# Causal mask by a product of constant rows, and row maxima of two heads at once, in a transformer block on one Trainium2 core

## What is computed

```python
xn = _layernorm(x, axis=-1)
q = (xn @ wq + bq).reshape(B, S, 16, 16); k = ...; v = ...
q = _apply_rope(q, cos, sin); k = _apply_rope(k, cos, sin)
scores = jnp.einsum('bhqd,bhkd->bhqk', q, k) / jnp.sqrt(jnp.float32(HEAD_DIM))
causal = jnp.where(jnp.tril(jnp.ones((S, S), jnp.float32)) == 0, -1000000000.0, 0.0)
attn = jax.nn.softmax(scores + causal, axis=-1)
s = jnp.einsum('bhqk,bhkd->bhqd', attn, v) -> (B, S, 256) @ wo + bo
g = _silu(((silu(xn @ wg.T) * (xn @ wu.T)) @ wd.T))
return x + s * g
```

## Time and profile before

| | us |
|---|---|
| median of 3 runs | 557.97 (557.56 to 561.14) |
| profiled execution: span | 562.5 |
| TensorE busy | 506.4 (90%) |
| VectorE busy | 461.9 (82%) |
| ScalarE, GpSimd busy | 332.2 (59%), 292.6 (52%) |

### The profile page before, as it was taken

One profiled execution on the slowest core, in us unless ns is written; L12 is line 12 of the kernel. 1 busy time (PEld: TensorE's weight loads), 2 busy tenths in 40 slices (PEclk: granted clock), 3 DMA queues, 4 the chain that ended last, 5 costly groups with the idle time before them and its releaser, 6 DMA issues.

```text
span 562.5 us, 11714 instructions
## 1 busy us (share of the span) xinstructions
PE 506.4 (90%) x3717; PEld 349.5 (62%) x3717; DVE 461.9 (82%) x1460; ACT 332.2 (59%) x682; POOL 292.6 (52%) x407
## 2 busy tenths in 40 slices
PE   0716989999999999979999999999999999999994
PEld 0614767566657677657866777676757775654753
DVE  3484897998799897976889897999799789998623
ACT  2257245676576657654586657674777556765750
POOL 2090059469263498344972499356854583422620
PEclk9977999999999999988999999999999999997996
DMA  5559624436307723383436733583436463652021
GB/s 194 183 157 241 120 71 140 116 98 166 67 4 197 196 65 115 116 176 109 108 123 145 195 63 115 149 182 110 134 101 151 113 173 115 128 124 60 4 77 38
DMA packets 47839, 69.47 MB, mean 124 GB/s; under 512 B 5496, under 2 KB 22776, under 8 KB 47776
## 3 DMA queue, kind: packets, MB, share of 16 engines
q1 hardware_dynamic: 46688, 67.62, 45.7%
q10 hardware_dynamic: 1088, 1.05, 0.6%
HBM read 38.11 MB, written 29.36 MB: 120 GB/s over the span
## 4 chain that ended last, share of the span: by engine, by line
PE 66%; DVE 15%; issue 5%; DMA 5%; SPq 4%; ACT 2%; POOL 2%; ACTq 0%; DVEq 0%; POOLq 0%
PE ps_w L544 36%; PE ps_w L556 15%; PE ps_o L648 10%; DVE ps_w L877 8%; PE ps_w L657 2%; SPq L517 2%; SPq L501 1%; DMA gate<-L_attn_wo 1%; ACT probs L767 1%; DVE row_max L877 1%; PE ps_w L663 1%; PE ps_w L569 1%; DMA k_st<-parts_k 1%; DVE high_low L865 1%; DVE hid L910 1%
## 5 line engine op out<-in xcount | busy, mean ns | idle before, releaser
L877 DVE CUSTOM_DVE_ANT_0 ps_w<-ps_w,cst 128x512 f32<-128x512 f32 (+3 forms) x512 | 235.3, 520 | 20.3 <-PE ps_w L556 19.4
L767 ACT ACTIVATE probs<-ps_w 128x512 f32<-128x512 f32 (+1 forms) x384 | 179.8, 535 | 63.8 <-PE ps_w L556 62.5
L959 POOL TENSOR_SCALAR_AFFINE_SELECT probs<-probs 128x256 f32<-128x256 f32 x256 | 108.5, 439 | 170.2 <-ACT probs L767 169.3
L544 PE MATMUL ps_w<-xt_hi,wgu_hi 128*128 128x512 f32 x192 | 84.1, 438 | 2.6 <-DVE row_max L877 1.1
L648 PE MATMUL ps_o<-probs,vals 128*32 128x512 f32 (+3 forms) x1024 | 84.6, 444 | 0.1
L556 PE MATMUL ps_w<-k_st,q_st 48*128 48x512 f32 (+3 forms) x512 | 80.0, 363 | 3.9 <-DMA k_st<-parts_k 1.8
L556 PE MATMUL ps_w<-q_st,k_st 52*128 52x512 f32 (+3 forms) x512 | 76.9, 354 | 4.4 <-DMA q_st<-minus_max 2.9
L544 PE MATMUL ps_w<-xt_lo,wgu_hi 128*128 128x512 f32 x192 | 76.8, 400 | 0.0
L556 PEld LDWEIGHTS ps_w<-k_st,q_st 48*128 48x128 f32 x512 | 45.0, 188 | 43.4 <-issue 28.1
L877 DVE DVE_READ_ACCUMULATOR2_ANT row_max<- 128x1 f32 x512 | 71.4, 139 | 0.0
L556 PEld LDWEIGHTS ps_w<-q_st,k_st 52*128 52x128 f32 x512 | 44.7, 187 | 32.4 <-issue 14.8
(11 more groups left out here) (98 smaller groups left out, 879.5 us busy)
## 6 DMA issues: line engine op xcount, KB each, us to landing
parts_q<-high_low SPq DMA_DIRECT2D x48, 256.0 KB, 3.1
q_st<-parts_q SPq DMA_DIRECT2D x64, 192.0 KB, 3.6
k_st<-parts_k SPq DMA_DIRECT2D x64, 192.0 KB, 4.6
parts_k<-high_low SPq DMA_DIRECT2D x42, 256.0 KB, 3.1
xn<-L_attn_x SPq DMA_DIRECT2D x8, 512.0 KB, 5.5
res<-L_attn_x SPq DMA_DIRECT2D x8, 512.0 KB, 4.0
q_st<-minus_max SPq DMA_DIRECT2D x256, 4.0 KB
result<-res SPq DMA_DIRECT2D x8, 512.0 KB, 5.1
```

Source lines behind the costliest of these rows:

```text
L544: last = pe.matmul(dst, w, m, start=(i == 0), stop=(i == len(terms) - 1))
L767: nc.scalar.activation(probs[:, (pair % 2) * SLOTS + slot, col:col + WIDTH[c]], w_of(kind, b, 3 * pair + c // 2, c % 2)[:, 0:WIDTH[c]], AC ...
L877: last = nc.vector.tensor_tensor_reduce(out=ps[:, col:col + w], in0=ps[:, col:col + w], in1=cst[:, C_MASK + SEQ - w:C_MASK + SEQ], scale=1 ...
L959: nc.gpsimd.affine_select(out=v, in_=v, compare_op=ALU.is_ge, fill=0.0, base=0, pattern=[[0, 2], [1, P]], channel_multiplier=-1).then_inc( ...
```

## The change

1. The mask of A is no longer added by VectorE. `causal` (128 by 384, constants, loaded as `mask_rows` and rounded once by ScalarE) has 64 rows for each head. In `masked_scores` every step of A ends with one more matmul per head, which adds the product of constant rows to the diagonal tile of each query tile: 128 columns in step 0, 256 in step 1 (both diagonals lie side by side), 128 in step 2. Both heads' banks are reported full together, by the last of these.
2. The maxima are plain `tensor_reduce` instructions. Where the two banks of a step are neighbours, one instruction takes both heads; else each head has its own. `a_taken` is raised once per step instead of once per bank, so both banks are let go together. TensorE's order and its banks are as before, but for the two heads the lower bank is the first now.
3. `row_max` is laid out so that its transpose holds 8 rows per head of a pair, MD needs 2 transfers of 8 rows each into one row of `q_st` per head, and B works with 49 rows. A row of ones in `k_st` (2 transfers at the start, from a memset) takes the place of the selector rows (8 transfers).
4. VectorE's list has 24 A items per batch instead of 48. The lists of TensorE, ScalarE, GpSimd and SyncE are the same.

```diff
 def scores / new masked_scores (TensorE)
+            def masked_scores(b, i):
+                pair, d = divmod(i, 3)
+                dst = [take_bank("A", b, i, 0), take_bank("A", b, i, 1)]
+                tiles, col_masked, masked = A_TILES[d]
+                for t, col in tiles:
+                    for h in range(2):
+                        pe.matmul(dst[h][:, col:col + (t + 1) * P], q_st[64 * h:64 * h + STACK, pair, t * P:(t + 1) * P],
+                                  k_st[64 * h:64 * h + STACK, pair, 0:(t + 1) * P], start=(col == 0), stop=False, skip_group_check=True)
+                for h in range(2):
+                    last = pe.matmul(dst[h][:, col_masked:col_masked + masked], causal[64 * h:64 * h + 64, 0:P],
+                                     causal[64 * h:64 * h + 64, P:P + masked], start=False, stop=True, skip_group_check=True)
+                done(last, "A")
...
+A_TILES = [([(3, 0)], 3 * P, P), ([(2, 0), (0, 3 * P)], 2 * P, 2 * P), ([(1, 0)], P, P)]
...
 B on TensorE
-                        need(pe, max_placed[g % 2], 128 * (2 * b + g // 2 + 1))
+                        need(pe, max_placed[g % 2], 32 * (2 * b + g // 2 + 1))
...
-                           lambda p, h, t, r: (q_st[64 * h:64 * h + r, p, t * P:SEQ], SEQ - t * P), STACK + 4)
+                           lambda p, h, t, r: (q_st[64 * h:64 * h + r, p, t * P:SEQ], SEQ - t * P), STACK + 1)
...
 MD on SyncE
-                    for tt in range(TT):
-                        for a in range(2):
-                            sp.dma_start(q_st[64 * a + STACK:64 * a + STACK + 4, 2 * i:2 * i + 2, tt * P:(tt + 1) * P].bitcast(F32),
-                                         minus_max[32 * tt:32 * tt + 4, i % 2:i % 2 + 1, :].bitcast(F32).broadcast_to([4, 2, P]))\
-                                .then_inc(max_placed[i % 2], 16)
+                    for a in range(2):
+                        row = q_st[64 * a + STACK:64 * a + STACK + 1, 2 * i:2 * i + 2, :].bitcast(F32).rearrange("o n (t c) -> o (n t) c", c=P)
+                        sp.dma_start(row, minus_max[32 * a:32 * a + 2 * TT, i % 2, :].bitcast(F32)).then_inc(max_placed[i % 2], 16)
...
 A on VectorE
-                    for h, qt, col in A_PARTS[c]:
-                        w = (qt + 1) * P
-                        hh = 2 * (pair % 2) + h
-                        last = nc.vector.tensor_tensor_reduce(
-                            out=ps[:, col:col + w], in0=ps[:, col:col + w], in1=cst[:, C_MASK + SEQ - w:C_MASK + SEQ],
-                            scale=1.0, scalar=-3e38, op0=ALU.add, op1=ALU.max, accum_out=row_max[:, g % 2, qt, hh:hh + 1])
+                    for t, col in A_TILES[d][0]:
+                        of_pair = row_max[:, g % 2, 0:64].rearrange("p (a c) -> p a c", a=2)[:, :, 4 * (pair % 2) + t]
+                        if second == first + 1:
+                            last = nc.vector.tensor_reduce(of_pair, ps_all[:, first:first + 2, col:col + (t + 1) * P], AX.X, ALU.max)
+                        else:
+                            for h, at in enumerate((first, second)):
+                                last = nc.vector.tensor_reduce(of_pair[:, h:h + 1], ps_w[at][:, col:col + (t + 1) * P], AX.X, ALU.max)
                     last.then_inc(a_taken, 1)
...
 the table of VectorE's order, one line of it
-        A12.6 A13.6 A14.6 A15.6 A16.6 A17.6 LO0.7 DN1.6 A18.6 A19.6 A20.6 A21.6 A22.6 A23.6 ON3.5 LO1.7 AT1.5 A24.6 A25.6 V0.7 A26.6
+        V1.7 A15.6 A16.6 G0.7 A17.6 U0.7 LO3.7 ON0.6 A18.6 HL0.7 A19.6 G1.7 A20.6 U1.7 G2.7 A21.6 OP0.5 A22.6 A23.6 U2.7 HL1.7 OP1.5 ON1.6
```

More of the change, by code:

```diff
@@ L45, in shape_constants, with causal_rows @@
     by_row = lambda t: np.tile(t.T, (HEADS, 1))
[L46 to L53, removed]
-    for a in range(2):
-        for s in range(2):
-            sel[4 * a + 2 * s + a, s, :] = 1.0
-    return sel.reshape(8, 2 * SEQ)
+    return np.concatenate([np.eye(P, dtype=np.float32), by_row(np.cos(freqs)), by_row(np.sin(freqs))], axis=1).astype(np.float32)
+def causal_rows():
+    of_q, of_k = np.zeros((P // 2, P), np.float32), np.zeros((P // 2, P), np.float32)
+    for r in range(P // 2):
+        of_q[r, 2 * r], of_q[r, 2 * r + 1] = 2.0 ** MASK_STEP, 2.0 ** -MASK_STEP
+        of_k[r, 2 * r] = -2.0 ** (-2 * MASK_STEP)
+        of_k[r, 2 * r + 1] = -2.0 ** (MASK_NEAR - MASK_STEP)
+        of_k[r, 2 * r + 2:] = -2.0 ** (MASK_NEAR + MASK_STEP)
+    return np.concatenate([np.tile(of_q, (2, 1)), np.tile(of_k, (2, 2))], axis=1)
 B_PARTS = [[(h, kt, col) for kt, col in part] for part in ([(0, 0)], [(1, 0), (3, 384)], [(2, 0)]) for h in range(2)]
-A_PARTS = [[(h, TT - 1 - kt, col) for h, kt, col in part] for part in B_PARTS]
+A_TILES = [([(3, 0)], 3 * P, P), ([(2, 0), (0, 3 * P)], 2 * P, 2 * P), ([(1, 0)], P, P)]
 WIDTH = [SEQ, SEQ, SEQ, SEQ, SEQ // 2, SEQ // 2]
@@ L186 @@
[L186 to L189, removed]
@@ L255, in __init__, with build @@
             assert len(banks) == WORK[kind][1]
-            for j, at in enumerate(banks):
-                full[first] += 1
-                kinds[kind] = kinds.get(kind, 0) + 1
+            for j, at in enumerate(sorted(banks) if kind == "A" else banks):
+                if j == 0 or kind != "A":
+                    full[first] += 1
+                    kinds[kind] = kinds.get(kind, 0) + 1
                 self.of[kind, b, i, j] = (at, full[first], seen.get(at))
                 seen[at] = (kind, kinds[kind])
-def build(nc, x, wq, bq, wk, bk, wv, bv, wo, bo, w_gate, w_up, w_down, consts, selectors, out):
+def build(nc, x, wq, bq, wk, bk, wv, bv, wo, bo, w_gate, w_up, w_down, consts, mask_rows, out):
     with ExitStack() as ctx:
@@ L301, in build @@
         k_st = sb("k_st", [P, PAIRS, SEQ], F32R)
-        row_max = sb("row_max", [P, 2, TT, 32], F32)
+        row_max = sb("row_max", [P, 2, P], F32)
+        causal = sb("causal", [P, 3 * P], F32R)
         minus_max = sb("minus_max", [P, 2, P], F32R)
@@ L479, in do @@
                 elif kind == "SL":
[L480 removed]
+                    sp.wait_ge(ones_set, 1)
                     for a in range(2):
[L482 to L484 removed]
+                        sp.dma_start(k_st[64 * a + STACK:64 * a + STACK + 1, :, :].bitcast(F32),
+                                     h_hi[0:PAIRS, 0, :].bitcast(F32)).then_inc(ones_placed, 16)
                 elif kind == "RL":
@@ L810, in do @@
                     nc.vector.memset(spread, 0.0).then_inc(set_once, 1)
+                    nc.vector.memset(h_hi[0:PAIRS, 0, :].bitcast(F32), 1.0).then_inc(ones_set, 1)
                 elif kind == "WC":
```

102 lines of the change are left out of this document (45 added, 57 removed).

## The result

The changed kernel takes 574.01 us (median of 4 runs, 570.72 to 574.91), the kernel before on the same chip 557.92 (557.56 to 561.14): ratio 1.0256, 95% interval 1.0209 to 1.0304. It is 2.6% slower. The forecast was 566.5 us, slower, within 552 to 584.

The account below looks back on a forecast made before the run. TensorE was taken as the fullest engine, VectorE close behind. Terms 18 - 7 + 4 - 6.5 = +8.5 us gave 571.0 us in the profiled execution; scaled to the runs, the forecast was 566.5 us, range 552 to 584.

Parts of the forecast that it names:

- 1 mask products: Three more pairs of matmuls on TensorE per head pair, 0.29 us each of 64 head pairs: +18 us.
- 2 plain maxima: VectorE's maxima as 437 instructions for 512 save 31 us of its busy time; the chain shortens by 7 us.
- 3 banks held longer: Both heads' banks go free together behind the step's last reduction, so TensorE waits longer: +4 us.
- 4 two transfers: SyncE's six fewer issues per group remove a 3.1 us wait and 3.4 us lost at low clock: -6.5 us.
- Rival B: All 15 us of TensorE's waits for maxima go, paying for the mask: 554.5 us in the runs, chance 0.22.
- Rival C: Latency binds, the mask falls into TensorE's gaps and is free: 543 us in the runs, chance 0.13.
- Rival D: The mask's small matmuls hide no weight loads: up to 52 us instead of 18, 600 us in runs, chance 0.13.
- Rival E: With all steps on neighbouring banks, VectorE's maxima would give -9 instead of -7, moving the sum by 2 us; no chance given.
- The signs: Profile marks: batch 1.5 to 3 us longer, VectorE down some 30 us and below 77%, q_st wait gone, full clock around 250 us.

Follow-up runs that it names:

- mask_alone: The changed kernel with the old kind of maximum (adding the cosine table instead of the mask) and banks let go per head: 579.02 us, ratio 1.0323.
- two_transfers: The kernel before with only part 3 of the change (new row_max layout, 2 transfers for 8, row of ones): 559.12 us, ratio 0.9973.
- head_by_head: The changed kernel with one plain reduction per head and tile (512 in all), each head's bank let go at once: 573.92 us, ratio 1.0232.
- no_mask: The changed kernel without its mask products, maxima over unmasked scores: 560.60 us, ratio 1.0006.
- before_again: The kernel before, unedited, run and profiled a second time: 560.18 us, ratio 1.0006, span 557.7 us.
- late_release: The kernel before with a_taken raised once per A step, so both banks go together: 574.18 us, ratio 1.0238.
- mask_twice: The changed kernel with every mask product issued two times: 589.46 us, ratio 1.0532.
- neighbours: The changed kernel with new bank numbers, so all 192 A steps have neighbouring banks and 256 reductions take both heads: 566.79 us, ratio 1.0113.

## Why the prediction was right, and what was off

In us, by the ratios. The four kernels form a chain from before to after, so their differences must add up to the whole: 19.6 - 5.1 + 1.3 - 1.5 = 14.3. "+-" is the interval worked out from those of the ratios, and another chain would split the whole otherwise (the mask costs 14.0 +- 3.1 when it is taken out of the changed kernel).

| term | forecast | bounds | measured, from |
|---|---|---|---|
| 1 mask products | +18 | 15, 52 | +19.6 +- 2.9, mask_alone less two_transfers |
| 2 plain maxima | -7 | -15, 0 | -5.1 +- 4.5, head_by_head less mask_alone |
| 3 banks held longer | +4 | 0, 19 | +1.3 +- 4.6, after less head_by_head |
| 4 two transfers | -6.5 | -6.5, 0 | -1.5 +- 1.5, two_transfers |
| sum | +8.5 | | +14.3 +- 2.7 |

- **The direction and its cause** hold. TensorE was nearly full, the mask went onto it, and 0.29 us a pair was right to the step: 0.06, 0.17, 0.06. "Nothing hides this" was a little too strong: beside no_mask, gaps take in 2 us.
- **The term that failed is 4.** I took a wait of 3.1 us and 3.4 us of half clock from one execution and put them in the sum at their full size. I had named the lower bound ("the wait is of this execution only"), and before_again, without the wait, bears it out: alone, the transfers gave 1.5 us, and the interval reaches to nothing. This is 5 of the 5.8 us between sum and result; the other terms miss by less than their intervals and partly against each other, which is luck. A sign was at hand: the span of 562.5 lay above every run timed then.
- **Terms 2 and 3** came out -3.8 together, forecast -3. Apart they depend on company, which my sum didn't allow for: held banks cost 13.3 us with the old, slower maxima (late_release) and 1.3 or 1.0 with the plain ones, with and without the mask. Plain maxima pay 5 us with the mask and nothing without. My 19 us bound held. That the slower maxima make the difference is argued, not shown: the order in which the two banks go free differs too. Both parts act at the same places, as at the first G in four batches, where a bank is late.
- **Rival B** (the stalls pay): the waits of weight loads for maxima fell from 16.4 to 10.7 us, not to nothing; the batch is longer than 60.4. **Rival C** (the mask is free) is refuted by no_mask, mask_alone and mask_twice. The Trainium skill's page Perfetto Trace Analysis (Identifying the Most-Contended Engine) goes by MFU and the weight loads' share. MFU was not worked out here; taken by the 62% of weight loads alone, there was room. The runs disagree: 14.0 to 19.6 us, where the starts give 0.29 x 64 = 18.6. **Rival D** (bare loads, up to 52 us): the starts and 19.6 us stand against it.
- **Rival E**: 2 us forecast, 8 measured by the ratios, of which the single instruction has at most 5.7 and, at a like clock, some 1 to 3. Whether it is undersized stays open.
- **The signs**: the batch is 1.6 to 1.8 us longer (1.5 to 3 asked); SyncE's wait for `minus_max` grew from 63.8 to 96.5 us; mask pairs stand 0.06 us before what follows, as said, and 0.17 where the sign said 0.12 and the sum 0.17; no wait for `q_st` and full clock around 250 us, but before_again had this too (waits of 0.6 us in all), so the sign told nothing of term 4. VectorE's busy time fell by 19 us, not 30, and its share to 78%, not below 77. The rows of the maxima alone fell by 23 us (235.3 to 151.0 + 61.5), and other rows grew by some 4, lines 392 and 868 above all. The rest of the 31 us that starts show is most likely records reaching beyond the next start. Maxima run at 1.05 ns a column.

## What to carry to other kernels

In this kernel, work moved from a nearly full engine onto the fullest one cost nearly its whole distance from start to start there (14.0 to 19.6 us, where the starts say 18.6), and of what it freed little came back: 5 us of 31, or nothing, most likely since hardly anyone waited for it. Price both by starts, not by the records' lengths or busy shares; here records of 0.23 to 0.34 us stood for 0.06 to 0.17. Before a stall of one profile goes into a sum, compare its span with the timed runs, or take a second profile of the same kernel. And before a difference of a few us goes to an edit, set the granted clocks of the runs beside each other.

## What was not expected of the hardware

- The same program gave spans of 562.5 and 557.7 us; the longer one held 7 us with the granted clock at 0.52 behind a 3.1 us wait, the shorter ran them at 1.00.
- Twelve runs of one program (neighbours) were granted mean clocks of 0.965 to 0.984 and took 575.0 to 563.3 us: 12 us, as much as most edits here moved.
- The stretch at half clock near 510 us is in both profiles of before and in the changed kernel (slice 37 of its clock row reads 7, before_again's 6). With the mask twice it is gone (only the third, the fourth and the last slice are below 9); why wasn't tried. Of its three other runs none had so high a mean clock (0.968 to 0.973; the profiled one 0.983), so it need not be gone in each:

```profile
PEclk9968999999999999999999999999999999999997
```

- Letting go of the first bank of each A step later by the second head's maxima (some 0.4 to 0.8 us, and in 8 steps by another item), with no work added, cost 2.4% of the whole kernel (late_release).
